# New order strings for the five engines of an audio-tower kernel

## The reference, cut to what matters

```python
h = tok(x)                       # taps, relu, batch norm over all rows
h = h + attn0(layernorm(h))      # 8 heads, softmax, band of 0.1 around the diagonal
h = h + ffn0(layernorm(h))       # 8 experts of 256, top 2 of a softmax gate, erf gelu
h = h + attn1(layernorm(h))      # 8 heads, linear causal attention (elu + 1)
h = h + ffn1(layernorm(h))       # norm, causal softmax attention of 2 heads, then 8 experts of 512,
                                 # full softmax gate, tanh gelu
```

## Time and profile before

| what | us |
|---|---|
| median of 3 runs | 4318.03 |
| lowest, highest | 4313.71, 4323.68 |
| span of the profiled execution | 4319.1 |
| first stage | to about 169 |
| first round | about 169 to 402 |
| 30 middle rounds | about 402 to 4168 |
| last round | about 4168 to the end |

### The profile page before, as it was taken

The page is one execution under the profiler, slowest core; times in us unless marked ns, Lnnn a source line. Parts: engine busy times, 40 slices in busy tenths (PEclk is TensorE's granted clock), DMA queues, the critical chain, the costliest instruction groups (busy, mean ns, idle before and its releaser), DMA issues.

```text
span 4319.1 us, 104773 instructions
## 1 busy us (share of the span) xinstructions
PE 4066.8 (94%) x41344; PEld 3009.8 (70%) x41344; DVE 3367.6 (78%) x8878; ACT 2784.5 (64%) x4796; POOL 2596.6 (60%) x2494
## 2 busy tenths in 40 slices
PE   7678999999999999999999999999999999999998
PEld 3346777777777777777777777777777777777766
DVE  3357888888888888888888888878888887888876
ACT  3235766666676666667666666766666676666654
POOL 2034666666666666666666666666666666666656
PEclk9779999999999999999999999999999999999999
DMA  4200000011100001110000111000101100010000
GB/s 149 68 27 28 18 18 29 28 30 30 30 19 24 22 28 30 30 30 18 23 23 28 30 30 30 23 26 16 30 28 30 30 23 26 16 30 28 28 16 6
DMA packets 136939, 127.62 MB, mean 30 GB/s; under 512 B 28928, under 2 KB 135360, under 8 KB 136448
## 3 DMA queue, kind: packets, MB, share of 16 engines
q1 hardware_dynamic: 136448, 120.91, 9.6%
HBM read 71.05 MB, written 49.55 MB: 28 GB/s over the span
## 4 chain that ended last, share of the span: by engine, by line
PE 56%; DVE 24%; ACT 6%; POOL 5%; issue 4%; DMA 3%; SPq 2%; ACTq 0%; DVEq 0%; POOLq 0%
PE pf L1301 9%; PE pf L1303 8%; PE pf L1302 8%; PE pa L1561 8%; DVE h L1285 4%; PE pa L1447 3%; DVE hid_hi L1266 3%; PE pa L1543 3%; PE pa L1346 2%; PE pa L1433 2%; POOL inv_norm L650 2%; PE pa L1301 2%; ACT xn L726 2%; PE pa L1641 2%; PE pa L1303 2%
## 5 line engine op out<-in xcount | busy, mean ns | idle before, releaser
L660 POOL TENSOR_TENSOR hid_lo<-hid,hid_hi 128x504 f16<-128x504 f32 x1536 | 1835.5, 1212 | 775.8 <-DVE hid_hi L1266 775.8
L886 ACT ACTIVATE hid<-pf,vec 128x504 f32<-128x504 f32 x1536 | 1014.7, 680 | 505.5 <-PE pf L1303 356.9
L1301 PE MATMUL pf<-w_hi,hid_hi 128*126 128x128 f16 x6144 | 1133.7, 224 | 10.7 <-DVE h L1285 10.2
L1303 PE MATMUL pf<-w_hi,hid_lo 128*126 128x128 f16 x6144 | 1115.8, 221 | 0.0
L1302 PE MATMUL pf<-w_lo,hid_hi 128*126 128x128 f16 x6144 | 1115.4, 221 | 0.0
L1301 PEld LDWEIGHTS pf<-w_hi,hid_hi 128*126 128x126 f16 x6144 | 844.1, 137 | 153.5 <-issue 53.2
L1302 PEld LDWEIGHTS pf<-w_lo,hid_hi 128*126 128x126 f16 x6144 | 843.8, 137 | 28.5 <-issue 0.2
L1266 DVE CAST hid_hi<-hid 128x504 f16<-128x504 f32 x1536 | 845.4, 573 | 8.2 <-ACT hid L886 2.7
L1303 PEld LDWEIGHTS pf<-w_hi,hid_lo 128*126 128x126 f16 x6144 | 845.2, 138 | 0.0
L1285 DVE SCALAR_TENSOR_TENSOR h<-pf,gates,h 126x128 f32<-126x128 f32 x2048 | 574.1, 342 | 155.2 <-PE pf L1303 152.6
L616 POOL TENSOR_TENSOR pt<-pt,band 126x262 f32<-126x262 f32 x512 | 351.2, 707 | 527.6 <-ACT pt L773 527.4
(11 more groups left out here) (208 smaller groups left out, 7486.8 us busy)
## 6 DMA issues: line engine op xcount, KB each, us to landing
qk_spread<-terms SPq DMA_DIRECT2D x224, 126.0 KB, 2.5
qk_spread<-terms SPq DMA_DIRECT2D x192, 63.0 KB, 2.3
y_scratch<-hid SPq DMA_DIRECT2D x32, 252.0 KB, 2.1
y_in<-y_scratch SPq DMA_DIRECT2D x32, 252.0 KB, 3.2
terms<-qk_hi SPq DMA_DIRECT2D x32, 252.0 KB, 2.5
terms<-qk_lo SPq DMA_DIRECT2D x32, 252.0 KB, 2.6
qk_spread<-terms SPq DMA_DIRECT2D x32, 252.0 KB
terms<-ot_hi SPq DMA_DIRECT2D x32, 252.0 KB, 2.4
```

Source lines behind the costliest of these rows:

```text
L660: nc.gpsimd.tensor_tensor(hid_lo[:, c % 8], hid[:, c % HIDS], hid_hi[:, c % 8], ALU.subtract).then_inc(hid_lo_done[c % 2], 1)
L886: nc.scalar.activation(hid[:, c % HIDS], pf[:, c % 2, 0:TOK], func, bias=vec[:, bias:bias + 1]).then_inc(F["hid_ready"], 1)
L1301: nc.tensor.matmul(out, ah, bh, start=start, stop=False, skip_group_check=skip)
L1303: return nc.tensor.matmul(out, al, bh, start=False, stop=stop, skip_group_check=skip)
```

## The change

The whole diff:

```diff
--- before.py
+++ after.py
@@ -156,41 +156,41 @@
 SPREAD0, SPREAD1 = 6 * 16, 9 * 16
 
 
-SP_START = ("qqqqqqqhhhhaaaaaaaaaaaaaaaaaaaaaaaaaaaaaohhaaoalhhqqqooqohohhhqqqhhaaaaaahaaoololhaooaalllolaaaa"
-          "alloooolallllallaaaaaaalllhhaaoaaaaahlollllollqqhhololoqqlhlhlllhlhhhqllhoolllllhqhoohloolhlqool"
-          "lhohholhl")
-SP_ROUND = ("lohoholhhllahaaloaolhohhaooaalllllllhohohhhahlaaalolaahhohllolaaolaoohhlaalohlalaoaahalhhhaaooal"
-          "hhooalllqhohohhohllolaaaaoloooohhlqqqhhhoahoohohqlholllololqhlhlhhlohholoqloolohhooooll")
-SP_END = ("lllllloohlhlohllhlolllooollhhhhooohlhollohllohhhhohlhlllllhhhhohoohhhllohoolllloooolhllllllllhlo"
-          "ohlhoolhohhhhhlhhhoolhoooloohhhoohoooooohohhhoooohhhhohhhhohhhohoooooooooooo")
-POOL_START = ("qqqqqqqaaaaaaaaaaaaaaaaaaaaaaaaaaaaahhhhhahhhahaqqhqqhhhhhhoqqoqaaaaalalaoolaaoallaolalalalaalal"
-          "aaaloololaalaaallllhaaaooalllolohooolhllaoaallolqqhhholhoollllohqlllqhhhhohoohlhlllohqqlohlllloo"
-          "hqooholhl")
-POOL_ROUND = ("ollhhhllhaloaahaaolhalhllaloahaloaahhahooahlolhallllaahoaahhohaaaahhohloaholohlalahholaallooooll"
-          "hqooohlhhlloohoohlolooohooloaaahololhoohhhoallhqqqhhhloohllhlaoolhhhlohloohlolqhqooqlll")
-POOL_END = ("llhllloolhoooooohhlhlhhollllollllllohoolohhllhhhlholllhllhohoohhoholloooolllohhohlolllhhllolllho"
-          "hhhhhhhhohhooohoololoooohlhhooohholhholholoohhhhhhohoohhohohhhhooooolohooooo")
-ACT_START = ("qqqqqqqaaaaaaaaaaaaaaaaaaaaaaaaaaaaoaohhhoaohaaqhhqqhhqhhhohholhqqqaaaaahhlalaalalllaalaallloaal"
-          "aalaaaoalaalaooollllaalahhloaooaoaaalhooqqllllhhhololhlllhhlooqqholloholhlloolllhlohlqlooqhlhllq"
-          "hoohholhl")
-ACT_ROUND = ("lhaaohahloaalhlolhhholhahlolahhoalahooaallllooaoahohlllhhhooolaolloaallaahohaalhoalhhhlahaoalhao"
-          "lhohhhoollhooolohoaooalqaaahhalhhlhhllhlolooolooqqqoooloahlllhqloooohhqloohhlqlhholhhll")
-ACT_END = ("hhlhhoollolllohhhooolholllhllolohhlllolohlhoohoohllhlollollhloohloohololohlhohlhloohlhllhloooolo"
-          "llolhlhllllolhhlhoooooohhohhhhhhhohhhoolhhohohoohhoohhhooohhohhohoohohoooooh")
-DVE_START = ("qqqqqqqaaaaaaaaaaaaaaaaaaaaaaaaaaaaoaahhhhhaoahqhhqoooohqhqhhooqqoohhoqohhoooolaaaaaallaalllaala"
-          "lallalaaallalaaaallaalllaalaaaallaahaholqlhlllhholqllhhlooolohllhlhqqlhooolllllholhoqohlhqolollh"
-          "qhohholhl")
-DVE_ROUND = ("laohalohhoalooohloalllhhoahoahohalahallolohhaoollaalohlhlhhalaahllaololhhaaooaalaoahlhaaoholhhoo"
-          "olhoalhlaaohqhholhollaoahoaoolhahoolhlohlollqhollqqhholollhahlooqqhlohqloolhhlohhoohlhl")
-DVE_END = ("lhlhhohlollollohlohoololohhlhloollllhlohhlolhohlhlllllolhlhoohllooholohollhholohlllhhlollhoolloo"
-          "oolhhlllolohhoholhhhlhohooohhhooohhhoooohhhhhoooohhohohhohhhoooohhoohhohoooo")
-PE_START = ("qqqqqqqaaaaaaaaaaaaaaaaaaaaaaaaaaaahhhhaahoaahohhqqoqoqhhoohhhhoolooqqhhqoolooooaaaaaalaalllalaa"
-          "laalalalallaalaaalallllaaalaahlhhlaaaaallollhohllhhlqqhhollqlhqooohlhllqhlhololllloolhoolqholoqh"
-          "llohholhl")
-PE_ROUND = ("lhhoalhhaoaoloahlohloaoohlhhlaooahlahohalolhalahllaaoolahollhholallhhalaaolaoloahhaolahhlhoohaoo"
-          "laahlhhlaohaoohlolqhoohalolaaohaoohhhoqqqlholhalhloqlolhlolollhhlooqlhhqololhhoohhoolll")
-PE_END = ("lhlhhhoohlllolhohoooohollhlhllollohlhllhhlolhlolhllhllolllhohoohlloooloolhhholhhhollolollhhllllo"
-          "ololoololhhllhhlhohhohohohhooohhohhooohohhohhooohhhoohohohhhoooohhhhoooooooo")
+SP_START = ("oqaaaaahoqhaqoqooqqqaaoolhqllqohhahahqoqaaaaaaqaqaoaaaqhqllhoaholhaaaaolqahlolllhlaalahollhahaol"
+            "hhalllhqoallalohoalaohaoaaalalolhlolallaaqalhlahhooaolhhhlalalolqloahaahllallaolloalhlahalhhahao"
+            "alaoaqqha")
+SP_ROUND = ("looooaahhhoohohoallalahhalqhaohloaooalaohahhahalolhhhhhoahhlloloaalllqollalhoohohholhhohalahlqhl"
+            "allhoaoaholahalllollhooollahqoahalhlhhoahqllqoollloohohoholoqholoaholoalaollollhaoolhhh")
+SP_END = ("hhloohololhhohhloohohohlohhlohollohlhlollhhhlooohlloloohohoolohlohoolhllhlolhoohhlhhohhoolooholl"
+          "hohhohohhhlooololoohhlhohlhoolllohhohlohhoooolhholooholllhhhhhlollhoohllolol")
+POOL_START = ("ooqqqqaqaaaaaaaaaaaaqaaaaaaaqaaaoohhqhooaahaqhahhooaahqqhhaahoaohahqaoaahoahhlaqqaalllqaallaaoao"
+              "llqoaaalllalalalaaaaahllolllollaoqlhlollalollahollhohhhlhllqohlooholhlllohaloalhqlolqoaloaolhhhh"
+              "lhqlhlhla")
+POOL_ROUND = ("olqlhoahhollhhallooaalllohalahhlahhhaalhlooaoallllahahloaaloooohallahaaalhoolaohhaoooqohaholhooo"
+              "llhalhlhooohoolhlahqloholaooooahohaholhhhaalhoholoqhaqolhhlhaqlhlholholhlohlohlllolhqlo")
+POOL_END = ("lllolhllhlllooooohllohoholhlhlhollhoohlhlhooollhlooohollolhhooohoolohllllhlhooohlohlohhoooooohho"
+            "loholohoolhohhhlhlolhhhlhhhohohlolohoohhhohhhhohhhlhloohooolohlhlolohhlooohh")
+ACT_START = ("aaaaqaqqqqaqaqaaaoaaoaaaaaooaaaooaaaaqaaahqqahhaahaahhqhahhhaahoaohqolahaqaohoqhhloallllallaaola"
+             "oaolaaoqollaalaalloaaalllalolaolalaolaqlaahoolhlohahqhlalhlhhllhlaohqhhoqlhlollllqllolhhlllohlqh"
+             "olohlhhol")
+ACT_ROUND = ("hoohhoahlalhoalololohhoaahlohalhhaohqloahohllalhaalaaohoolllolaallaahloohaolaolaohoohlohaloolhll"
+             "aahhahhlaaoqlhlhhoqloolahhohaaaohlolhhollllqlohlohoooollhohahqhhllqohlholqohlhollhohoao")
+ACT_END = ("ohooolhlhooolollooohhhllhhohollllollohhololhooollollololhohhlhlhlllhhhooollhlooohlhohooloooholoh"
+           "llholloollolololohollhhlhhlhhollooohhhoohohhlhhhohhohohhhhohhohhhooohhhooohh")
+DVE_START = ("qqqqqqqaaaaaaaaaaaaaaaaaaaaoaqaaqaaaaaahhhqahahohohoqohoqhohohohqhohqooohahoooolaaalalalllaaalaa"
+             "aalllaalaaallallaalaalalllalalqaalalqalhhalllhhaoohlhohhllahoooqqhlollolqohlolhllqllhlhollolhhql"
+             "hohhlloho")
+DVE_ROUND = ("loaholhaahloholollhaooohahlahaolhahlhalaoaoohoaloalhllahllaoohlaooaollhlahhalhalhalaalholqhohall"
+             "hlahqohoolhaaohhooloolaalhaooholaohlolohlhlhqoqohlhlolhloqhhoohlolhqlholhoqolohhooahhll")
+DVE_END = ("ololhhhllolloohhoolollhhlhhlllhohololloloohllllohlhhlhlolhhlloohlhoolhlhooololhhlollhoolllhollho"
+           "loohlloohhhlollhlhhhlohoohhoohohohohhoohohhohohohhhhoooohohoohhohhohooooohoo")
+PE_START = ("qqqqqqqaaaaaaqaaqaaaaaaaaaaaaaaalaaaaaahhhhahaoqhoqhoohhohohhoohqhqooqoohalhooooaaaalalllaaaqqla"
+            "laalalalaalalalaallaalaallalallalaalahhlhlqalhhlooahhqlhoholohhlhooahqlolqllolhhlollllololholqll"
+            "hohhlhloo")
+PE_ROUND = ("llhhoahhaohaolohallhooloqholahhoahoahoalhhalholahloalaolalhoalloalhallaqaolahlahlhaolahloolhhqll"
+            "oaoahhlaoohhlaoohloohaalholhhoaooahahalloolhqoholllqloohlhlhoohhloohlqholoqlolhohhloohl")
+PE_END = ("hollhholollhhlhhololhohohohllololloolhllhhlllhhlololhololhlolhhllhooholhhlollohoohoohlllhlloolll"
+          "loloolohhhhllohhololhhlhohhoohoohhohhooohhoohhohhohhooohohhoohoohhhoooohoooo")
 
 
 def chunks_of(kind, p):
```

## The result

The median of four runs is 4221.39 us (4218.90 to 4223.08) against 4319.29 (4313.71 to 4323.68) for the kernel before, a ratio of 0.978 with a 95% interval of 0.9766 to 0.9794. The gain is 98 us, 2.2%. The forecast was 4301 with a range down to 4232, so the direction was right and the size far off.

A forecast was written before the change was run, and what follows sets the result against it. TensorE, busy 4066.8 us, bounds the kernel; only its idle time can move. Saved 3.75 less added 3.3 is .45 us a round, 13.5 over 30, plus 3 in the first round: 4301 from 4318, range 4232 to 4350.

The forecast's parts named there:

- l28: Transposes of the second norm: the norm chain ends about .6 earlier against the same cover, saving .65 us a round.
- l47: Gate bias products: three steps placed ahead of them cover their wait, saving .6 us a round with the restart.
- l8: First products on the loaded terms: .9 more cover, mostly against a DMA wait, saves .3 us a round.
- ten small waits: Ten small TensorE waits, each with more cover in the new order: 2.2 us a round saved together.
- h31: TensorE waits for ScalarE's exp and two table loads, now behind four copies: .9 us a round added.
- l33: First score products, waiting for VectorE's q2t with less cover: wait from .75 to 1.6, +.85 us a round.
- l37, l38: P transposes: later exps add .3 us net; the step after them shows ScalarE's copy, adding .25.
- l6, a14, l21, l22, a21: Added waits: .3 us at the first, for a ScalarE step; .6 at the others together, mostly from thinner cover.
- Rival 1: GpSimd's subtractions hold ScalarE in front of the exps: slower by up to 1.2 us a round, 4337; chance .25.
- rival 2: Added waits at h31, l33 and l37 are one wait; if half of 3.3 stays, 4252 us; chance .18.
- Rival 4: ScalarE pauses a load's length after each of two table loads at h31: 77 us more, 4378; chance .02.
- First and last round: First: a chain starts up to 2.7 us earlier, 3 saved (0 to 6). Last: 0 (-3 to +3).

The follow-up runs named there:

- e5: Changed kernel with h34 on TensorE moved from ahead of the transposes l32 to between them and the first scores l33; 4196.2 us, 0.9726.
- e4: Changed kernel with VectorE's casts of h29 and h30 moved back ahead of the multiply l31; 4217.7 us, 0.9778.
- e6: Changed kernel with o29 on TensorE moved ahead of h31; 4202.2 us, 0.9737.
- e3: Kernel before with VectorE's cast of h29 moved behind the subtraction l28; 4362.7 us, 1.0115.
- e7: Changed kernel with ScalarE's exp a26 and its table load moved back ahead of l29's copies; 4248.6 us, 0.9841.
- e11: Changed kernel with the edits of e5 and e6 together and the END strings of the kernel before; 4188.3 us, 0.9711.
- e1: Kernel before with only the five ROUND strings new, START and END strings kept; 4223.3 us, 0.9794.
- e10: Kernel before with o46 and o47 on TensorE placed between the gate's transpose l46 and its bias products l47; 4312.9 us, 0.9997.

## Why the prediction was right or wrong, point by point

Measured from start to start of TensorE's instructions, mean of 27 middle rounds, the interval into the step and inside it (a step's neighbours alone move it by up to .15):

| term | predicted | measured |
|---|---|---|
| l28 | -.65 | -.74 |
| l47 | -.6 | -.52 |
| l8 | -.3 | -.42 |
| ten small waits | -2.2 | -2.55 |
| l29 (no term) | 0 | -.49 |
| a12 (no term) | 0 | -.28 |
| h31 | +.9 | +.78 |
| l33 | +.85 | +.04 |
| l37, l38 | +.55 | +.16 |
| l6, a14, l21, l22, a21 | +.9 | +.13 |
| others (a0, o32, o40 and more; the switch) | +.1 | +.73 |
| sum | -.45 | -3.16 |

The others' +.73 (a0 and o40 +.30 each, o32 +.24) is not accounted for: no run isolates it.

**Right:** the saved side, 3.75 against 4.2, read from waits and cover (within the ten small waits the total came out, and not each part: l34 alone gave .93 of it); h31's new wait, in place and in size (.83 on its boundary, forecast .9); the loads ahead of the Gelus, still 217. Rival 1 did not come: after k2t the Gelus of h33 and h34 start without a wait for GpSimd. ScalarE's timeline around l29's last copy and around k2t:

```profile
1571.05 0.48 ACT L838 COPY v<-pa 126x384 f32<-126x384 f32 x1
1571.54 1.28 ACT L732 ACT_TABLE_LOAD   x1
1572.84 0.23 ACT L732 ACTIVATE lge<-lg 126x32 f32<-126x32 f32 x1
1573.09 1.28 ACT L886 ACT_TABLE_LOAD   x1
1574.38 1.25 ACT L886 ACTIVATE hid<-pf,vec 128x504 f32<-128x504 f32 x2
...
1581.81 0.58 ACT L843 COPY pt<-pa 128x504 f32<-128x504 f32 x1 [2.17 <-PE pa L1603]
1582.28 1.26 ACT L886 ACTIVATE hid<-pf,vec 128x504 f32<-128x504 f32 x2
```

**The step that failed** is the added side, 3.3 a round where 1.1 came, and l33 first: "l33, the first score products ... +.85". It took 2.7 from the end of l31 to q2t's end against TensorE's .9, as if TensorE began l32 the moment l31 ended, as before, and took only .2 off for h31's delay. In the changed kernel l31 ends at 1579.20 and l32 begins at 1580.74, 1.5 later:

```profile
1577.97 1.23 DVE L1215 TENSOR_TENSOR v<-v,inv_norm 126x1024 f32<-126x1024 f32 x1
1579.11 0.75 DVE L1266 CAST hid_hi<-hid 128x504 f16<-128x504 f32 x2
1579.78 1.12 DVE L1285 SCALAR_TENSOR_TENSOR h<-pf,gates,h 126x128 f32<-126x128 f32 x4
1581.38 0.74 DVE L1218 TENSOR_SCALAR pt<-pa,qk_gain 128x504 f32<-128x504 f32 x1 [0.48 <-PE pa L1603]
```

```profile
1580.74 1.03 PE L1603 MATMUL pa<-ident,v 126*128 126x126 f32 x8
1582.53 0.49 PE L1614 MATMUL pa<-pt 64*126 64x126 f32 x4 [0.76 <-ACT pt L843]
```

The casts and accumulations stand between l31 and q2t as the prediction says, 1.8 us of them, but they lie beside a30 and h34 on TensorE, and q2t even waits .48 for l32. What l33 waits for is k2t, because nothing stands between l32 and l33: .76, which e5 filled and e4, with a slower multiply, didn't touch. Two things put l31's end that far ahead, and they also make up the .40 that l32 had waited for l31 before. The multiply takes 1.23 and not the 2.16 of the earlier trace rows, since no subtraction of GpSimd runs beside it. TensorE is held .77 at h31 first. The prediction took a duration from the old neighbourhood and carried it into the new one. Neither was decisive alone: e4 takes the first away and e6 the second, and the scores' group stays at 25.0 and 25.2 us. Both away at once weren't run.

The prediction also misread the old order. It had l33 wait for q2t there (2.1 against .9 + .64), but the earlier trace rows put 19.2 of the scores' 24.0 us down to ScalarE's k2t and 0.3 to q2t. In the kernel before, ScalarE took a Gelu ahead of k2t, and that Gelu waited for GpSimd. The round of the earlier trace rows, TensorE and then ScalarE:

```profile
1628.64 1.08 PE L1603 MATMUL pa<-ident,v 126*128 126x126 f32 x8 [0.18 <-DVE v L1215]
1630.97 0.49 PE L1614 MATMUL pa<-pt 64*126 64x126 f32 x4 [0.61 <-ACT pt L843]
```

```profile
1629.68 0.68 ACT L886 ACTIVATE hid<-pf,vec 128x504 f32<-128x504 f32 x1 [1.40 <-POOL hid_lo L660]
1630.26 0.57 ACT L843 COPY pt<-pa 128x504 f32<-128x504 f32 x1
```

In the mean of 27 middle rounds k2t ended 2.19 after l32's start and q2t 1.88. In the new order no such Gelu stands ahead of k2t, which ends 1.64 after l32's start. That is .55 earlier, against the .64 of cover that went with h37, so l33's wait stayed as it was.

**l29** was left out of the ten waits. Its .52 was VectorE's subtraction (L1199), 1.28 beside GpSimd's and .68 alone; e3 removed it by one moved cast. And "h31 ... +.9" priced the exp's new place on one side only: e7 shows that it keeps 1.54 off l29.

**l37 (+.3), l38:** o33's accumulations do stand between the masks and cost their 1.1 there. But o32 and o33 on TensorE stand there too, where only h38 stood, so l34 takes .93 less (of the ten small waits' 2.55, for which the prediction took 2.2 together). This is the account of the trace; no run isolates it. l38's +.25 came, as +.22. For l6, a14, l21, l22 and a21, +.9 was put on covers thinned by .6 or so that still sufficed.

**Rivals.** The time lies nearest to rival 2 (4252), and even beyond it, but its reason is wrong: e6 took h31's wait away and .43 of .69 came out at the end, where "one wait" says nothing would. The added waits were not merged; most were never there. (Once both are covered they do meet: .71 and .43 singly, .94 together in e11.) Rival 4, a pause after each table load, did not occur: in the rows above the exp follows its load's start by 1.30, the Gelu by 1.29.

**First and last round:** -3 and 0 forecast, -5.9 and +3.7 in the profiles. The first is the START strings', by the two groups of profiles under e1, and twice what was forecast. For the last the trace of the change shows l8 waiting 3.09 for the loads of the terms (.15 before), and right behind that wait the granted clock at .50 for 13.7 us (6.8 in the last round before, earlier in it). But e5 and e7, with the same END strings and waits of 2.8 and 2.9, have last rounds within .7 of the one before, so the cause stays open.

## What to carry to other kernels

An order written by hand is priced by the arrival times of both sides: shift every start along the new order first, and let each operation's length depend on what runs beside it. A gain at one step of a tuned order is not a gain of the round: four edits that took a real wait away on the old order gave nothing or lost up to 4.8%, because a consumer, or a collision, stood right behind; look for the moved step's next consumer on every engine. Which chain ends a wait is read from its row: the prediction reckoned q2t where the row named k2t. Once the order is good, the cheap gain is a filler where TensorE waits for a copy or a bank: here one between a transpose and the product that needs its copy and one ahead of h31 brought a further .94 us a round. On the old order the same kind of move (e10) gave nothing.

## What the runs showed of the hardware

VectorE's multiply, subtraction and casts between SBUF tiles took longer beside a subtraction or the squares of GpSimd. The multiply l31 took 2.16 from 1626.42 to 1628.58 in the kernel before; GpSimd's subtraction began at 1626.36 and takes 1.14 alone, to 1627.50, after which 1.08 remain, about the 1.23 that the multiply takes by itself. GpSimd was held up too, with 3.22 for two subtractions:

```profile
1626.36 3.22 POOL L660 TENSOR_TENSOR hid_lo<-hid,hid_hi 128x504 f16<-128x504 f32 x2
```

In e3 an operation of .19 took 1.31 and ended .04 after the squares beside it. Operations that read PSUM, such as the masks (L1223, 546 and 547 ns in the two kernels) or the accumulations (L1285, 342 and 341), kept their lengths, and so did the sums of squares (L1205), which read one SBUF tile: 1.21 and 1.22 in the two kernels, with a subtraction beside them in every middle round. Not all of GpSimd's work holds VectorE up. In the changed kernel two products of two SBUF tiles each, L1018 and L1020, lie beside GpSimd's power (L650) in all thirty middle rounds and take .42, as they do before with nothing beside them:

```profile
1575.04 2.90 POOL L650 TENSOR_TENSOR inv_norm<-ss_eps,minus_half 126x16 f32<-126x16 f32 x1 [0.45 <-DVE ss_eps L1209]
...
1576.32 0.42 DVE L1018 TENSOR_TENSOR ob<-ob,earlier 126x256 f32<-126x256 f32 x1
```

The Trainium skill (SBUF — State Buffer, Who interferes with whom) says that a VectorE instruction with two SBUF inputs contends with a GpSimd instruction that reads SBUF, and the later one waits out the other. The traces agree for the subtractions and squares (1.23 against 2.16, .68 against 1.28, .19 against 1.31); beside the power, which reads SBUF too, they show no such wait, and the measurement decides. By that rule the prediction's 2.16 depended on the neighbour.

VectorE's busy time fell by 109 us (3367.6 to 3258.5) with the same instructions. Most of it lies in three groups: the casts, which read one SBUF tile (L1266, mean 573 to 521 ns; .42 alone and 1.36 beside GpSimd's subtraction in the earlier trace rows), the multiply (67.1 to 39.2 us) and l28's subtraction (39.5 to 21.9). e4 shows that such a collision costs nothing where another wait ends later.
